# Side work placed by the TensorE time left free in a piece, and the value products one quarter earlier

## What is computed

```
x = x + attn_a(layernorm(x))   # scores = -distance of 3-d positions / 4, causal; one map for all 16 heads
x = x + ffn(layernorm(x))      # sigmoid(xr Wr) * (relu(xk Wk)^2 Wv), xr and xk mix a token with the one before
x = x + attn_b(layernorm(x))   # 16 heads of 16 channels, causal softmax(q k / 4) v
x = x + ffn(layernorm(x))
```

## Time and profile before

| | |
|---|---|
| median of 3 runs | 2317.15 us (2314.3 to 2317.2) |
| the profiled execution | 2316.06 us |
| its span, first to last instruction | 2314.3 us |
| mean granted TensorE clock | 0.92 |
| first attention matmul (L811) | at 208.2 us |
| last one | at 2225.4 us |
| the fifth image's turn (192 quarters) | 1261.1 to 1534.0 us |

### The profile page before, as it was taken

One profiled execution on the slowest core, in us unless ns is written; L12 is line 12 of the kernel. 1 busy time (PEld: TensorE's weight loads), 2 busy tenths in 40 slices (PEclk: granted clock), 3 DMA queues, 4 the chain that ended last, 5 costly groups with the idle time before them and its releaser, 6 DMA issues. The chain is left out here.

```text
span 2314.3 us, 32515 instructions
## 1 busy us (share of the span) xinstructions
PE 1929.1 (83%) x9842; PEld 936.3 (40%) x9842; DVE 1417.5 (61%) x4173; ACT 1254.3 (54%) x2673; POOL 1024.2 (44%) x1074
## 2 busy tenths in 40 slices
PE   4477888888988899788987889888887889988986
PEld 3344343334433354324543345333443335432423
DVE  2336677567676666666765666756656666677642
ACT  0623654675537555394545755366554855555563
POOL 4454354335642455334743266423654246422414
PEclk8677899989998899989999899998999899999998
DMA  3006011310132111211122011231113111141100
GB/s 96 0 20 117 1 28 42 69 28 15 43 85 34 28 29 53 67 29 28 33 67 64 13 29 37 76 63 28 28 37 83 28 28 28 43 87 29 29 19 19
DMA packets 64347, 97.27 MB, mean 42 GB/s; under 512 B 15655, under 2 KB 58029, under 8 KB 58030
## 3 DMA queue, kind: packets, MB, share of 16 engines
q1 hardware_dynamic: 64174, 95.20, 18.6%
HBM read 61.09 MB, written 33.55 MB: 41 GB/s over the span
## 5 line engine op out<-in xcount | busy, mean ns | idle before, releaser
L852 ACT ACTIVATE pt<-exp_bank 128x512 f32<-128x512 f32 (+3 forms) x1536 | 742.5, 494 | 806.5 <-PE exp_bank L822 797.0
L867 DVE CUSTOM_DVE_ANT_0 max_bank<-max_bank,mask 128x128 f32<-128x128 f32 (+3 forms) x1024 | 500.3, 502 | 495.2 <-PE max_bank L811 478.2
L822 PE MATMUL exp_bank<-qs,ks 98*128 98x512 bf16 (+3 forms) x1536 | 523.8, 347 | 72.5 <-ACT pt L852 66.3
L811 PE MATMUL max_bank<-ks,qs 96*128 96x512 bf16 (+3 forms) x1536 | 525.0, 349 | 24.3 <-DVE piece_max L870 17.2
L870 DVE TENSOR_REDUCE piece_max<-max_bank 128x1 f32<-128x512 f32 x512 | 342.9, 686 | 164.7 <-PE max_bank L811 161.5
L837 PE MATMUL o_bank<-pt,v 128*17 128x512 f32 (+3 forms) x3072 | 346.2, 525 | 8.0 <-ACT pt L852 3.0
L889 POOL TENSOR_SCALAR_AFFINE_SELECT pt<-pt 128x512 f32<-128x512 f32 x256 | 170.1, 664 | 404.2 <-ACT pt L852 403.8
L353 POOL TENSOR_SCALAR xh<-xs,mv,rstd 128x256 f32<-128x256 f32 x256 | 322.6, 1266 | 10.0 <-PE side L379 3.8
L822 PEld LDWEIGHTS exp_bank<-qs,ks 98*128 98x128 bf16 x1536 | 153.9, 101 | 353.4 <-ACT pt L852 229.5
L811 PEld LDWEIGHTS max_bank<-ks,qs 96*128 96x128 bf16 x1536 | 154.7, 101 | 257.9 <-issue 102.1
L544 PE MATMUL side<-vp,p 128*128 128x260 f32 x576 | 185.2, 450 | 33.7 <-ACT p L473 18.3
(11 more groups left out here) (94 smaller groups left out, 2243.0 us busy)
## 6 DMA issues: line engine op xcount, KB each, us to landing
parts_dram<-parts SPq DMA_DIRECT2D x64, 384.0 KB, 2.6
qs<-parts_dram SPq DMA_DIRECT2D x192, 128.0 KB, 7.0
ks<-parts_dram SPq DMA_DIRECT2D x32, 384.0 KB, 4.8
xs<-in_L_attn_a_x_dram SPq DMA_DIRECT2D x16, 512.0 KB, 4.3
ks<-parts_dram SPq DMA_DIRECT2D x32, 256.0 KB, 5.5
out_dram<-xs SPq DMA_DIRECT2D x16, 512.0 KB, 3.1
ks<-parts_dram SPq DMA_DIRECT2D x32, 128.0 KB, 5.9
qs<-neg_maxT SPq DMA_DIRECT2D x64, 8.0 KB, 1.9
```

Source lines behind the costliest of these rows:

```text
L811: pe.matmul(max_bank[u % MAX_BANKS][:, 0:k1 - k0], qs[r][0:KROWS, j, P * tile:P * (tile + 1)], ks[r][0:KROWS, j, k0:k1], start=True, stop= ...
L822: pe.matmul(exp_bank[k % EXP_BANKS][:, 0:q1 - q0], ks[r][:, j, P * kt:P * (kt + 1)], qs[r][:, j, q0:q1], start=True, stop=True).then_inc(s ...
L852: act.activation(pt[:, e % 2, j, 0:q1 - q0], exp_bank[k % EXP_BANKS][:, 0:q1 - q0], ACT.Exp, scale=SCALE).then_inc(exp_done, 1)
L867: dve.tensor_tensor_reduce(scores, scores, mask[:, HALF - w:HALF], 1.0, LOWEST, ALU.add, ALU.max, piece_max[:, j, m:m + 1]).then_inc(max_f ...
```

## The change

The planner now counts in *ticks*. A group still has 48 ticks on its 48 quarters, but they lie unevenly: `LEFT` gives each quarter a room of 2700 columns less its own attention columns, 300 at least, and `moment` turns a tick into a quarter and an eighth within it. Two ticks can fall in one quarter, which then takes two side parts in their order. Starts, spacings and the distance times are set anew. The value products go from the last quarter of the next piece (`GH - 1`) to the third (`GH - 2`), and `attention_time` counts them there. The generator of attn_a is cut into independent ones (values, positions, distances, residuals; values, positions and attend on PE), so that a position job can stand between two values jobs. No instruction is added or left out.

```diff
-ATT1, FFN2, FFN4, PROJ3 = -44, 50, 82, 114
-FIRST = {("att1", 0): -220, ("ffn2", 0): -126, ("proj3", 0): -74,
-         ("att1", 1): -28, ("ffn2", 1): 66, ("proj3", 1): 114}
+ATT1, FFN2, FFN4, PROJ3 = -46, 35, 75, 112
+FIRST = {("att1", 0): -240, ("ffn2", 0): -154, ("proj3", 0): -88,
+         ("att1", 1): -36, ("ffn2", 1): 50, ("proj3", 1): 112}
-LN_HALF = {"att1": 8, "ffn2": 16, "ffn4": 16, "proj3": 12}
+LN_HALF = {"att1": 12, "ffn2": 20, "ffn4": 20, "proj3": 10}
-PIECE_TIME = [2 + (q1 - q0) // P for _, q0, q1 in KEY_PIECES] + [5, 5, 5]
-PIECE_AT = [34 + sum(PIECE_TIME[:p]) for p in range(NP + 4)]
+PIECE_TIME = [max(3, 1 + 5 * (q1 - q0) // HALF) for _, q0, q1 in KEY_PIECES] + [5, 5, 5]
+PIECE_AT = [32 + sum(PIECE_TIME[:p]) for p in range(NP + 4)]
 JOBS = {"ln": [("tr", c, 12 + c, 1, 1, 2) for c in range(NC)],
-        "att1": [("values1", t, 16 + t + TPH * (t // TPH), 1, 1, 2) for t in range(NT)] +
-                [("positions", k, 29 + k, 1, 1, 1) for k in range(6)] +
+        "att1": [("values1", t, 16 + 2 * t + TPH * (t // TPH), 1, 1, 2) for t in range(NT)] +
+                [("positions", k, 26 + k + 7 * (k // 3), 1, 1, 1) for k in range(6)] +
                 [("attend", t, PIECE_AT[attended_from(t)] + 2, t // 2 + 1, 1, 2) for t in range(NT)],
-        "ffn": [("keys", j, 24 + 2 * j, 2, 1, 1) for j in range(2)] +
-               [("receptance", j, 31 + 2 * j, 2, 1, 1) for j in range(2)] +
-               [("products", j, 36 + 2 * j, 2, 1, 2) for j in range(2)],
-        "proj3": [("project", j, 24 + 3 * j, 2, 1, 1) for j in range(8)] +
-                 [("values3", j, 26 + 6 * j, 2, 3, 2) for j in range(4)]}
+        "ffn": [("keys", j, 24 + 3 * j, 2, 1, 1) for j in range(2)] +
+               [("receptance", j, 30 + 4 * j, 2, 1, 1) for j in range(2)] +
+               [("products", j, 37 + 3 * j, 2, 1, 2) for j in range(2)],
+        "proj3": [("project", j, 24 + 4 * j, 2, 1, 1) for j in range(8)] +
+                 [("values3", j, 26 + 4 * j, 2, 1, 2) for j in range(4)]}
+def attention_time(u):
+    t, j = divmod(u, GH)
+    width = [k1 - k0 for _, k0, k1 in QUERY_PIECES][t % NP] + [q1 - q0 for _, q0, q1 in KEY_PIECES][(t - LEAD) % NP]
+    return width + (4 * ([q1 - q0 for _, q0, q1 in KEY_PIECES][(t - LEAD - 1) % NP] + 64) if j == GH - 2 else 0)
+LEFT = [max(2700 - attention_time(u), 300) for u in range(GH * NP)]
+TICK = [0]
+for u in range(QUARTERS + 200):
+    TICK.append(TICK[-1] + LEFT[u % (GH * NP)] * GH * NP / sum(LEFT))
+def moment(tick):
+    if tick < 0:
+        return tick
+    u = next(u for u, at in enumerate(TICK) if at >= tick - 1e-6)
+    first = next(k for k in range(tick, -2, -1) if k < 0 or u > 0 and TICK[u - 1] >= k - 1e-6)
+    return u + (tick - first - 1) / 8
...
     while parts or rows:
-        while rows and rows[0][0] <= u and min(free) <= u:
+        u = moment(tick)
+        while rows and rows[0][0] <= u and min(free) <= tick:
...
                 if last:
-                    emptied[key] = free[bank[key]] = u + delay[key]
-        u += 1
+                    free[bank[key]] = tick + delay[key]
+                    emptied[key] = moment(tick + delay[key])
+        tick += 1
...
-    WRITTEN_AT[k] = max(k + max(0, shift - (k - since) // 4), WRITTEN_AT.get(k - 1, BEGIN))
+    WRITTEN_AT[k] = max(moment(k + max(0, shift - (k - since) // 4)), WRITTEN_AT.get(k - 1, BEGIN))
...
-            if j == GH - 1 and 1 <= e <= PIECES:
+            if j == GH - 2 and 1 <= e <= PIECES:
...
             for u in range(BEGIN, END):
                 attention(u)
-                for entry in parts:
-                    while entry[0] <= u:
-                        entry[0] = next(entry[1], NEVER)
-                parts = [entry for entry in parts if entry[0] < NEVER]
+                while parts and (first := min(parts, key=lambda entry: entry[0]))[0] < u + 1:
+                    first[0] = max(first[0], next(first[1], NEVER))
+                    if first[0] == NEVER:
+                        parts.remove(first)
```

More of the change, by code:

```diff
@@ L130, in place @@
     quarters, bank, emptied, late = {}, {}, {}, []
-    free, before, shift, u = [BEGIN, BEGIN], BEGIN, 0, BEGIN
+    free, before, shift, tick = [BEGIN, BEGIN], BEGIN, 0, BEGIN
     while parts or rows:
-        while rows and rows[0][0] <= u and min(free) <= u:
+        u = moment(tick)
+        while rows and rows[0][0] <= u and min(free) <= tick:
             key = rows.pop(0)[1]
             k = free.index(min(free))
-            quarters[key], bank[key], emptied[key] = [u], k, u + 2
-            free[k] = u + 2
+            quarters[key], bank[key], emptied[key] = [u], k, moment(tick + 2)
+            free[k] = tick + 2
         if parts:
@@ L140, in place @@
             regained = max(0, shift - max(0, at - before) // 4)
-            if at + regained <= u and (k > 0 or min(free) <= u):
+            if at + regained <= tick and (k > 0 or min(free) <= tick):
                 parts.pop(0)
-                before, shift = at, max(regained, u - at)
+                before, shift = at, max(regained, tick - at)
                 late.append((at, shift))
@@ L159 @@
 BANK[0,], BANK[1,] = 0, 1
-END = max(EMPTIED_AT.values()) + 20
+END = int(max(EMPTIED_AT.values())) + 20
 WRITTEN_AT = {}
@@ L381, in pe_transposed, with dve_values1 @@
                 mm.then_inc(tr_full, 1)
-        def dve_att1(at, n):
+        def dve_values1(n):
             dve = nc.vector
-            def values(t):
+            for t in range(NT):
+                yield EMPTIED_AT["values1", "att1", n, 0, t]
                 dve.wait_ge(v1_full, 8 * n + t + 1)
@@ L407, in distance, with dve_residuals @@
                                          op0=ALU.max, op1=ALU.add).then_inc(dist2_ready, 1)
-            def residual(t):
+        def dve_residuals(n):
+            dve = nc.vector
+            for t in range(NT):
+                yield EMPTIED_AT["attend", "att1", n, 0, t]
                 bank = side_of("attend", "att1", n, 0, t)
@@ L416, in residual, with act_positions, act_distances @@
                                          op0=ALU.mult, op1=ALU.add).then_inc(x1_done, 1)
[L418 to L440 removed]
+        def act_positions(n):
+            for k in range(6):
+                h, c = divmod(k, 3)
+                yield EMPTIED_AT["positions", "att1", n, 0, k]
+                nc.scalar.wait_ge(pb_full, 6 * n + k + 1)
+                nc.scalar.activation(pb[:, c, HALF * h:HALF * (h + 1)], side_of("positions", "att1", n, 0, k)[:, :],
+                                     ACT.Copy).then_inc(pb_ready, 1)
+        def act_distances(at, n):
+            act = nc.scalar
             def square(p, c):
@@ L473, in transform @@
                     act.activation(p1[:, at:at + w], d, ACT.Exp, scale=-SCALE).then_inc(p1_exp, 1)
-            for k in range(6):
-                yield EMPTIED_AT["positions", "att1", n, 0, k]
-                positions(k % 3, k // 3)
             for p in range(NP + 1):
@@ L506, in pool_att1, with pe_values1 @@
                                        sq[:, p % 2, 1, 0:w], ALU.add).then_inc(sum_ready, 1)
-        def pe_att1(n):
+        def pe_values1(n):
             pe = nc.tensor
-            def values(t):
+            for t in range(NT):
+                job = "values1", "att1", n, 0, t
+                yield PARTS_AT[job][0]
                 if t % TPH == 0:
                     pe.wait_ge(xt_ready, 2 * LN_AT["att1", n, t // TPH] + 2)
-                bank = side_job(("values1", "att1", n, 0, t), vp_ready, 8 * n + t + 1)
+                bank = side_job(job, vp_ready, 8 * n + t + 1)
                 for c in range(NC):
@@ L518, in values, with pe_positions @@
                 mm.then_inc(v1_full, 1)
-            def positions(c, h):
+        def pe_positions(n):
+            pe = nc.tensor
+            for k in range(6):
+                h, c = divmod(k, 3)
+                job = "positions", "att1", n, 0, k
+                yield PARTS_AT[job][0]
                 pe.wait_ge(vp_ready, 8 * n + TPH * (h + 1))
-                bank = side_job(("positions", "att1", n, 0, 3 * h + c), pb_ready, 6 * n + 3 * h + c + 1)
+                bank = side_job(job, pb_ready, 6 * n + k + 1)
                 for t in range(TPH):
@@ L527, in positions, with pe_attend @@
                 mm.then_inc(pb_full, 1)
+        def pe_attend(n):
+            pe = nc.tensor
             for t in range(NT):
-                yield PARTS_AT["values1", "att1", n, 0, t][0]
-                values(t)
-            for k in range(6):
-                yield PARTS_AT["positions", "att1", n, 0, k][0]
-                positions(k % 3, k // 3)
-            for t in range(NT):
-                yield PARTS_AT["attend", "att1", n, 0, t][0]
+                job = "attend", "att1", n, 0, t
+                yield PARTS_AT[job][0]
                 m = t + 1 if t < TPH else TPH + t + 1
@@ L539, in pe_att1 @@
                 pe.wait_ge(p1_sel, NT * n + t + 1)
[L540 removed]
```

(2 more changed lines are left out.)

69 lines of the change are left out of this document (26 added, 43 removed).

## The result

| | before | after |
|---|---|---|
| median, 4 runs each | 2315.73 us (2311.38 to 2317.2) | 2459.09 us (2454.15 to 2464.87) |
| span of the profiled execution | 2314.3 us | 2463.1 us |
| mean granted TensorE clock | 0.92 | 0.90 |

The change makes the kernel slower: 1.0623 times the time before, interval [1.0595, 1.0652]. The forecast was 2330 us with 2270 to 2370 as its range. The sign was right; the size, 143 us, was ten times what was foreseen.

A forecast was written before the change was run, and what follows sets the result against it. ACT was taken to pace a turn's first group, PE and its waits the other three. The terms gave +2.4 us a turn, +17 for seven, less 3 at the start: +14 on 2316.06, so 2330 us, range 2270 to 2370.

The forecast's parts named there:

- Products a quarter earlier: Value products on PE: 56 of 383 sets would come late, a third of that lost, +1.9 us a turn.
- PE work leaves the PE-paced part: Third group of a turn: 5.9 us of PE work go to the first group, worth -6.5 us a turn.
- ACT work enters the first group: First, ACT-paced group: attn_a's late pieces add ACT work there, +3.0 us a turn, bounds 2 and 4.
- The clock rival: First group: more PE work may raise its granted clock from 0.79 to 0.95, 2302 to 2272 us; chance 0.15.
- Handovers: Side banks: waits for their emptying go from 24.4 to 26.0 us a turn, +1.6, bounds -3 and +4.
- Unevenness: Quarters of a piece: side parts fall unevenly on PE, +2.4 us a turn, bounds 0 and 6.5.
- Ahead of the first turn: Start of the kernel: values of half an image no longer delay its positions, -3 us, bounds -8 and +3.
- The sign: Whole kernel: slower, by 0.6%; chances slower 0.47, faster 0.40, same 0.13.

The follow-up runs named there:

- e1: Kernel before with only the value products moved from the fourth quarter to the third of the next piece; 1.0474 times the kernel before.
- e16: Kernel before with the value products one step later, behind the fourth quarter's side parts at the head of the next piece; 1.036 times the kernel before.
- e2: Kernel after with the value products back in the fourth quarter and counted there; 1.0115 times the kernel before.
- e12: Kernel before with both ffn stages started 6 quarters earlier; 1.0149 times the kernel before.
- e8: Kernel after with even ticks and the value products in the fourth quarter, new starts and spacings kept; 1.0134 times the kernel before.
- e10: Kernel after with old starts, spacings and distance times and products in the fourth quarter, uneven ticks kept; 1.0018 times the kernel before.
- e3: Kernel after with every tick one quarter long, new starts, spacings and earlier products kept; 1.0361 times the kernel before.
- e9: Kernel before with products in the third quarter, all side work one quarter earlier and ACT's `ot` copy two, maxima left; 1.0331 times the kernel before.
- e13: Kernel before with only the four off-diagonal product sets of each group moved to the third quarter; 1.0153 times the kernel before.
- e15: Kernel before with only the product set of piece 8 in each group moved to the third quarter; 1.0193 times the kernel before.
- e5: Kernel before with products in the third quarter, ACT's `ot` copy two quarters earlier and the maxima one quarter later; 1.0381 times the kernel before.
- e7: Kernel before with only the transposes of the maxima one quarter later; 1.0054 times the kernel before.
- e17: Kernel before with values1 jobs given a side bank only from the quarter after it is emptied; 0.9917 times the kernel before.

## Why the forecast was wrong, step by step

**Products a quarter earlier** is the step that failed. It had +1.9 us a turn, with 0 and 5.6 as its bounds. e1 measures it alone: over six turns the turn grows from 269.9 to 282.8 us, +12.9, and 112 us in all. 12.5 of the 12.9 are idle time of PE and 0.4 busy time, so a lower clock (0.93 for 0.94) has next to no share in it. The working was right up to the 56 late sets. Two things after it were not. That all but a third would replace waits at the banks was chosen between bounds with nothing in a row behind it: the waits before L837 rose by 6.2 us a turn, more than the upper bound, and all falls elsewhere together, of which 1.4 us before L516 is the largest, come to 4.5. And only the set's own start was looked at, not what lies behind its old place. That is the larger part: before the maxima +3.8 us a turn, before L658 (`wrT`) +2.8, before L718 +2.0, before L379 +1.4. Waits before the last three rise by 9.4 us a turn when the sets go the other way (e16), with no set late, so lateness of the sets does not make them. The step's upper bound should have counted the cover: 48 sets a turn, each with up to 0.98 us of PE work that stops lying over the chains of DVE and ACT, 47 us in all; what it was worth was 12.9.

**PE work leaves the PE-paced part**, -6.5 us a turn, did not come. In e2, the change without the products, PE is busy in the third group for 61.4 us and before for 65.6 (means over the four steady turns, from all matmul records), so the work left as counted. But PE's idle time in it rose from 7.4 to 14.7 us and the group is 76.1 us instead of 73.0. PE did not pace it by its work alone. 4.2 us of e2's idle time there stand before `wvT` (0.1 before) and 4.8 before L379 (2.0 before), both behind chains of other stages. Whether the work that left had covered these chains or the new spacings make them too tight isn't separated. e12, with the old spacings, is for the second: there the work leaves, the idle time stays within 0.5 us and the group does shorten, by 3.3 us for 5.2. What the term missed besides is what such work costs where it goes, 6.2 us for 3.5 in e12.

**ACT work enters the first group**, +3.0: e2's first group is 60.0 us for 56.9, the size that was foreseen, but not by its mechanism as far as the rows go: ACT is busy for 51.6 us of it in both kernels, and idle for 3.1 us more in e2. The agreement may be luck. **The clock rival** is out: that group's clock is 0.84 for 0.79 after, but the group is 7 us longer, and in e2 0.86 and 3 us longer. Nor does a group's clock go by PE's idle time in it: the fourth group of the earlier trace rows has the most, 14.4 of 75.4 us, and is granted 1.00.

**Handovers**, +1.6 with +4 as the upper bound: of the waits named, those of values1 fell (L516 by 1.7 us a turn) and those before the maxima rose, as foreseen; those before L944 fell. Missed were `wvT` (+3.9 us a turn, to 3.9) and L379 (+4.5, to 9.3), which wait for ffn and layer-norm chains. In e2 they stand at 4.2 and 6.6 us, in e8 at 4.2 and 8.9, in e10 at 3.0 and 7.4, and in e1 at 0 and 6.1. So the new times bring them, and so do uneven ticks alone; the products alone bring 1.4 us before L379 and nothing before `wvT`. All of the change but the products comes to +2.7 us a turn (e2) where the terms without the products gave +0.5: this much was missed by the rest.

**Unevenness**, +2.4, is +0.6 a turn alone (e10), and with the new times -0.8 (e2 against e8); L822's idle time fell where a rise was to show it. With the products in the fourth quarter it did no harm beyond that. Together with the products it does: after is 2.5% above e3. In the trace after, the maxima wait 9.1 us a turn, in e1 5.9 and in e2 4.3, now for side banks; that is where the two meet, as far as it was followed.

**Ahead of the first turn** 3 us less were foreseen. The first attention matmul comes at 212.2 us instead of 208.2.

**The sign** was right by luck more than by the working: the terms without the products gave +0.5 us a turn and came to +2.7 by other ways than foreseen, the one that carries most of the loss had +1.9, and the chances had 0.40 on faster.

**What stays open.** e9 still loses 78 us. Of the 67 us between the profiled executions its rows name 19 more before L837 (23 behind the select), 20 before L822, 11 before L718 and 5 before L658, and PE is busy for 13 more; before L910 12 more behind `neg_max` are made up for by 14 less behind ACT. Why these come isn't shown. e13's waits are named above, but not why its sets bring them. That lost cover is the cause is shown at the maxima (e15). For the waits before L658 it is argued: it rests on e1, e16 and e9, where the wait comes (24.9 us), comes (24.9) and goes (7.9) with the distance between products and side parts. For those before L718 and L379 nothing of the kind was run. Why the clock is a little lower after (0.92 for 0.94), and how much of PE's 3.0 us a turn of longer busy time it makes, wasn't measured either.

## What to carry to other kernels

When an instruction moves in an in-order list, price two places: where it goes, by what it will then wait for, and where it was, by the chains of other engines that it had been lying over; a set of 1.05 us moved by one quarter cost 46 us in 32 groups, 1.4 us each. A late wait should be taken whole, unless a row shows the wait that it replaces. In this kernel a rule against waits that the plan brings about itself (a bank used in the quarter in which it is emptied) was worth more than balance: it gave 0.8%, and 1.5% with uneven ticks, which alone gave nothing.

## What the runs showed that was not expected

The size of a wait in the list did not tell what its removal is worth. Taking 33 us of waits for `neg_max` away gave 7 us, since 30 us came back before L822 and L658 (e5), those before L822 with the shift itself, as e7 shows. Taking 18 us away before L516 gave 19, although L822's waits rose there too, from 66.3 to 79.5 us (e17). Over six turns e17 gains 3.2 us a turn, but only 0.6 of them as idle time of PE; 2.6 are busy time, with the same matmuls. By groups (means of the third to sixth turn) the fourth, in which the values1 jobs stand, is 2.7 us shorter and idles 2.8 less, so there the wait came back as time. The first idles 1.2 us more, before L822, and is shorter even so, since PE is busy for 1.8 less. What makes PE's busy time shorter there was not measured.
